# Taking the reader-less TensorE products out of the opening of a three-layer decoder kernel

## The reference, cut to what matters

```python
x = _layernorm(x + attn(x, ...))               # x: 64 sequences x 64 rows x 256
x = _layernorm(x + xattn(x, ctx, ..., 64))     # 8 heads, within |i - j| <= 64 of 256
x = _layernorm(x + ffn(x, w_gate_up, w_proj))  # ternary weights, silu(gate) * up, rms_norm

def attn(x):   # 16 heads of 16, rotary, layernorm of q and k, causal
    q = layernorm(x) @ Wq + bq; k, v = layernorm(x) @ Wkv + bkv
    q, k = ln(rotary(q)), ln(rotary(k))
    return softmax(causal(q @ k.T / 4)) @ v @ Wo + bo

def ternary_quant(w):  # groups of 64
    scale = max(mean(|w|), 1e-8); return round_to_minus1_0_1(w / scale) * scale
```

## Time and profile before

| what | value |
|---|---|
| median of 3 runs | 856.19 us |
| lowest, highest | 854.46, 863.31 us |
| the profiled execution's own time | 854.88 us |
| its span | 853.2 us |
| PE busy | 776.2 us (91%), 9593 instructions |
| DVE busy | 766.6 us (90%) |
| POOL, ACT busy | 692.5 us, 681.0 us |
| weight loads (PEld) | 464.0 us |
| share of line 538 in the chain of waits, first 220 us | 3.0% |

### The profile page before, as it was taken

The page is one execution under the profiler, slowest core; times in us unless marked ns, Lnnn a source line. Parts: engine busy times, 40 slices in busy tenths (PEclk is TensorE's granted clock), DMA queues, the critical chain, the costliest instruction groups (busy, mean ns, idle before and its releaser), DMA issues.

```text
span 853.2 us, 23669 instructions
## 1 busy us (share of the span) xinstructions
PE 776.2 (91%) x9593; PEld 464.0 (54%) x9665; DVE 766.6 (90%) x1503; ACT 681.0 (80%) x1331; POOL 692.5 (81%) x689
## 2 busy tenths in 40 slices
PE   5788899999999999999999999999999989889884
PEld 3345445555556665556666655556665556555442
DVE  5999997889999999999999999999999998889653
ACT  3367558678889899889888888999899888778864
POOL 5896578888989999999999999999999897465731
PEclk9999999899999999999999999999999999999999
DMA  8100211111333333333333333333333323334333
GB/s 263 39 25 13 58 39 40 27 35 43 70 67 62 70 77 70 76 71 76 76 66 75 67 62 70 76 74 71 67 76 71 70 64 70 70 64 82 64 76 85
DMA packets 125117, 58.00 MB, mean 68 GB/s; under 512 B 93072, under 2 KB 124048, under 8 KB 125008
## 3 DMA queue, kind: packets, MB, share of 16 engines
q1 hardware_dynamic: 125008, 56.49, 30.2%
HBM read 13.98 MB, written 4.19 MB: 21 GB/s over the span
## 4 chain that ended last, share of the span: by engine, by line
PE 69%; DVE 14%; ACT 7%; issue 3%; SPq 3%; POOL 2%; DMA 2%; POOLq 0%; DVEq 0%; ACTq 0%
PE ps L778 9%; PE ps L579 6%; PE ps L856 5%; PE ps L826 5%; PE ps L842 4%; PE ps L747 4%; PE ps L649 4%; PE ps L710 4%; PE ps L589 3%; DVE rowmax L3017 3%; PE ps L617 3%; PE ps L631 2%; PE ps L817 2%; PE ps L678 2%; PE ps L690 2%
## 5 line engine op out<-in xcount | busy, mean ns | idle before, releaser
L3017 DVE TENSOR_REDUCE rowmax<-ps 128x4 f32<-128x768 f32 x256 | 243.2, 950 | 10.1 <-PE ps L710 9.3
L1744 ACT ACTIVATE prob<-ps 128x768 f32<-128x768 f32 x256 | 207.3, 810 | 32.1 <-PE ps L747 31.9
L2508 POOL TENSOR_TENSOR hsum<-hsum,minus_half 128x32 f32<-128x32 f32 x32 | 175.9, 5495 | 11.0 <-DVE hsum L2942 10.9
L2533 POOL TENSOR_SCALAR_AFFINE_SELECT prob<-prob 128x512 f32<-128x512 f32 (+1 forms) x128 | 112.0, 875 | 24.6 <-ACT prob L1744 24.3
L2535 POOL TENSOR_SCALAR_AFFINE_SELECT prob<-prob 128x1024 f32<-128x1024 f32 (+1 forms) x128 | 114.3, 893 | 0.0
L778 PE MATMUL ps<-prob,v_pad 128*32 128x192 f32 x2048 | 97.2, 331 | 0.2 <-POOL prob L2535 0.2
L710 PE MATMUL ps<-k_rows,q_rows 31*128 31x192 f16 x1024 | 86.7, 247 | 9.1 <-DMA k_rows<-qk_lo 4.2
L747 PE MATMUL ps<-q_rows,k_rows 32*128 32x192 f16 x1024 | 86.5, 247 | 5.7 <-ACT prob L1744 5.4
L778 PEld LDWEIGHTS ps<-prob,v_pad 128*32 128x32 f32 x2048 | 60.3, 110 | 30.7 <-issue 17.1
L826 PE MATMUL ps<-wgu,xsplitT 128*128 128x512 bf16 x226 | 59.4, 380 | 12.0 <-ACT v_own L1653 9.1
L856 PE MATMUL ps<-wproj,hT 128*128 128x256 bf16 x512 | 62.5, 276 | 5.7 <-DVE y L3103 4.9
(11 more groups left out here) (162 smaller groups left out, 2025.8 us busy)
## 6 DMA issues: line engine op xcount, KB each, us to landing
v_swap<-v_own SPq DMA_DIRECT2D x64, 68.0 KB, 2.1
xin<-in_x SPq DMA_DIRECT2D x32, 128.0 KB, 2.2
enc<-in_ctx SPq DMA_DIRECT2D x32, 128.0 KB, 2.3
q_rows<-qk_hi SPq DMA_DIRECT2D x64, 64.0 KB, 2.0
k_rows<-qk_hi SPq DMA_DIRECT2D x64, 64.0 KB, 2.1
out<-yout SPq DMA_DIRECT2D x32, 128.0 KB, 2.0
prob<-in_w_guT SPq DMA_DIRECT2D x4, 512.0 KB, 6.4
q_rows<-qk_lo SPq DMA_DIRECT2D x32, 64.0 KB, 2.0
```

The costliest lines, as they stand in the source:

```text
L1744: copy(prob[:, 2 * c:2 * c + 2, :, :].rearrange("p u a b -> p u (a b)"), ps[:, STB:STB + 2, 0:2 * QW], ACT.Exp, scale=float(XD) ** -0.5).t ...
L2508: g.tensor_tensor(hsum[:, t.two, 1, :], hsum[:, t.two, 0, :], minus_half[:, :], ALU.pow).then_inc(S["head_pow3"], 1)
L2533: g.affine_select(out=lead, in_=lead, compare_op=ALU.is_ge, fill=0.0, base=BAND - 64 * kb, pattern=[[0, 8], [1, cut]], channel_multiplier=-1)
L3017: v.tensor_reduce(of_head[:, hq:hq + 2, 2 * row_of(ng):2 * row_of(ng) + 2], ps[:, MXB:MXB + 2, 0:2 * QW].rearrange("p j (a b) -> p j a b", ...
```

## The change

The function `keep_warm` and its 33 calls are removed, 165 products and 165 weight loads. All other instructions, their order and their waits stay; the lines behind move up, those of the functions by 5. Nothing changes on the other four engines. The diff, its calls cut to the first ones and the last:

```diff
@@ -532,11 +532,6 @@
                 last.then_inc(s_setup, 1)
 
-            def keep_warm(times):
-                pe.wait_ge(s_fold, 3)
-                for _ in range(times):
-                    mm(ps[:, OTB, :], identb[:, :], causal[:, :], start=True, stop=True)
-
             def sum_weights(n):
...
@@ -993,29 +988,21 @@
...
             do_qk_ps(tile[1])
-            keep_warm(5)
             sum_weights(0)
-            keep_warm(12)
             sum_weights(1)
             pe.wait_ge(S["v"], tile[0].at(1, 1))
             do_xnT_ps(tile[2])
-            keep_warm(12)
             pe.wait_ge(S["xnT"], tile[2].at(1, 1))
             do_qk_ps(tile[2])
-            keep_warm(7)
...
             do_s_ps(tile[2])
-            keep_warm(12)
             pe.wait_ge(S["s_sub"], tile[2].at(1, 1))
...
             do_mx(tile[2], 3)
-            keep_warm(3)
             pe.wait_ge(S["exp"], tile[0].at(8, 7))
```

More of the change, by code:

```diff
@@ L1009, in _ @@
             do_v_ps(tile[1])
-            keep_warm(8)
             pe.wait_ge(S["v"], tile[1].at(1, 1))
             do_s_ps(tile[0])
-            keep_warm(9)
             sum_weights(2)
-            keep_warm(10)
             pe.wait_ge(S["xn"], tile[3].at(1, 1))
             do_xnT_ps(tile[3])
-            keep_warm(6)
             pe.wait_ge(S["s_exp"], tile[0].at(1, 1))
@@ L1056, in _ @@
             sum_weights(4)
-            keep_warm(1)
             pe.wait_ge(s_vswap[tile[1].buf], tile[1].dma(2))
@@ L1134, in _ @@
             do_mx(tile[1], 1)
-            keep_warm(8)
             pe.wait_ge(S["max"], tile[1].at(8, 2))
             do_mx(tile[1], 2)
-            keep_warm(4)
             pe.wait_ge(s_vswap[tile[3].buf], tile[3].dma(2))
@@ L1147, in _ @@
             do_xproj_ps(tile[2])
-            keep_warm(2)
             pe.wait_ge(s_maxrow[tile[0].buf], tile[0].dma(1))
             do_st(tile[0], 0)
-            keep_warm(2)
             pe.wait_ge(S["max"], tile[1].at(8, 4))
```

## The result

The changed kernel took 872.5 us in the median of four runs (866.43 to 878.56), against 857.77 us for the kernel before beside it: ratio 1.0148, 95% interval 1.0087 to 1.0208. It is slower, since 1 lies outside the interval; whether by 2% is open. Every ratio and interval in this document leaves out executions more than 1.5% above the fastest one of the same kernel, while the medians given in us are over all executions. The profiled execution took 866.43 us, 11.5 us more than the profiled one of before (854.88). The calls of `keep_warm` were 32, not 33 as the text ahead says; the 165 products are right.

The account below looks back on a forecast made before the run. VectorE was taken to bound the opening. First gaps and 42 to 50 us cost 4.9 us, later falls at even chances 3.8, less 0.5 won: +8.2 on 854.88, so 863.1 us; range 853 to 873.

Parts of the forecast that it names:

- The bound and the pass-through: VectorE bounds the opening to 130 us; from 200 us both engines are full, so any loss is handed on whole.
- What it gives: VectorE's wait for tile 1's attention values at 78.58 us shrinks: 0.5 us won, bounds 0 and 6.3.
- The clock: Emptied gaps drop TensorE's clock: sure in the first two and at 42 to 50 us, even for shorter later ones.
- A: First gaps: q/k projection of tile 2 at 34.28 us runs at the low clock, VectorE waits, +1.5 us.
- B: Gaps of 42 to 50 us: transposes, tile 3's q/k projection and weight sums run slower, +3.4 us.
- C: Around 73 to 82 us: transposes, attention values and output projection slower, +2.1 us if the clock falls, at even chances.
- D: 102 to 110 us: tile 5's q/k projection and logits slower, +3.1 us if the clock falls, at even chances.
- E: 119 to 130 us: output projection and tile 6's q/k projection slower, +2.4 us if the clock falls, at even chances.
- rival 2: Clock stays low through nearly the whole opening, transposes not bringing it back: +18 us, 867 to 878 us; chance 0.17.
- rival 1: VectorE's own work hides the slower products in the opening: +0 to +4 us, 855 to 859 us; chance 0.20.
- 3 (faster): Clock does not fall in the opening and VectorE gets back 2.3 us of waits: 849 to 853 us; chance 0.08.
- 4 (nothing happens): Real work already keeps the clock level in the opening, so time stays 854.9 us; chance 0.03.

Follow-up runs that it names:

- the two half kernels: Kernel before with only blocks 10 to 32 (90 products) out: ratio 1.0131; with only blocks 1 to 9 (75) out: ratio 1.0039.

## Why the prediction was right, and where its sizes were off

**The bound and the pass-through** held. VectorE carries the opening, the engines are full from 200 to 680 us, and the lateness is handed on: 8.8 us at 182 and 9.4 at 680, between 8.2 and 9.7 on the way.

**What it gives** (0.5 us): nothing visible. The wait at 78.58 us grew from 0.51 to 1.58 us instead of shrinking.

**The clock.** "Sure in the first two gaps and in those of 42 to 50 us" held: at 24.9 and 45.4 us here, and likewise in both other kernels without the early blocks. "As even for the shorter ones later" was too low: there were three falls, at 76.1, 89.7 and 117.0 us. The reading behind it was short, too: the longest emptiness of before at the high level is not the 3.39 us of the earlier trace rows but the 4.31 us ahead of tile 30's down projection, and there the clock fell, at 842.65 us. Shown by the two half kernels: the late blocks' absence alone costs about 7.8 us up to 140 us, the early ones' about 3.1.

**A** was put at +1.5 and measured +1.6 (0.7 to 2.35 us late, of it a wait of 1.56); 1.35 was regained by 52 us, 1.0 of it because one instruction of VectorE (line 2889 of before) ran 0.73 us instead of 1.76. **B** was put at +3.4: the wait for the projection was 2.90 and that for the values 0.44, so 3.3, and the lateness grew by 2.9 between 52 and 58 us. The level did come back in time for the values (at 59.0 us), as assumed. **C**, +2.1 if it falls: it fell, +1.4 (3.8 to 5.2). **A fall at 89.7** was in no term and made +1.4 at the logits of tile 3 (5.2 to 6.6), of which 0.8 was regained by 114 us. **D**, +3.1 if it falls: the clock was 1.00 from 96.6 to 117 us and the cost nil. I had also misread: VectorE shows no wait before those logits; they ended at 109.52 us, just as it came free. **E**, +2.4 if it falls: +4.3 between 114 and 136 us, since the low level lasted 17 us and slowed the row-maximum products too, for which VectorE waited 2.1 us in one place; no price for those stood in the sum. All told 10.1 at 140 us, 8.8 at 182, against 8.2 forecast. That these are so near is partly luck: the falls behind 70 us were counted at half and three came, one of them unpriced, while D did not; 1.35 us of A and 0.8 later were regained, which the sum did not have; 0.7 us stem from before the change's place; and the 1.3 us between 140 and 182 come back because before has its own fall there.

**The remainder** is a term that I did not have. The sum stopped at 132 us and stood on one execution of before, 854.88 us, which had been lucky: its clock was 1.00 between 680 and 765 us, where seven of eight other kernels with the same end show falls. The kernel's own median over 90 executions is 860.6, 5.7 us above my base. The measured 872.5 us is 9.4 above the forecast 863.1, so this base is the larger part of it. The forecast said that "one execution can differ by as much as I forecast here" and still took 854.88 for its base. The rest, 3.7 us, is not placed: the loss itself is 8.8 us in the profiled execution, 8 to 11 between like ends and 12.7 by the ratio to before (7.5 to 17.8), against 8.2 forecast. The profiled execution is also the fastest of the changed kernel's four, and the three others had more of the lower clock (0.931 to 0.951 against 0.955); where they had it is not recorded. So the time stands near the upper end of the range (853 to 873), outside the forecast's own 859.3 to 866.9 and within what rival 2 had. By the time alone one would have picked rival 2; the trace says that it is the forecast's mechanism, and that the range held the result with half a microsecond to spare owes something to luck.

**The rivals.** 1 (VectorE's work hides it) is excluded by its waits of 13.7 us and by three falls behind 70 us. 2 (low through nearly the whole opening) did not come: the clock was low for 58 us of the opening, and came back four times before 97 us. The run from 53.5 us on held eight transposes (two groups of 1.1 us), a projection of 3.6 us and sums, and the level was back at 59.0. So the level did not stay away for the transposes' sake, which is what rival 2 needed. Whether they count toward it, as the Trainium skill denies in "TensorE: Matmul & The Clock Gate", section "PE-mode transpose", is not shown, since the projection may have brought it back, and none of my runs had transposes alone. 3 (faster) and 4 (nothing happens) are excluded. The statement of the Trainium skill, "TensorE: Matmul & The Clock Gate", section "What's actually happening", that the ramp costs under 1% of a typical kernel's span, and which would have given rival 1 or a loss under 8.6 us, is not what the centre of the measurement says, 1.5% (0.9 to 2.1), though the interval reaches below 1%. The level was lost five times in the opening here and not once.

## What to carry to other kernels

Products without a reader paid here where TensorE waits in gaps, the real work behind a gap is on the path, and the filler uses the whole array; fillers on a quarter of the rows were worse than none. Look for the gaps at both ends of a pipeline, where slots for tiles that are not there stand empty. And before a difference of 1% is forecast or explained, ask whether the profiled execution is a typical one: its mean clock beside that of the other runs tells.

## What the runs showed of the hardware that I had not expected

- The time of one and the same kernel spreads over 15 us (853.65 to 868.37 in 90 executions, each on one core, of four chips), and most of it goes with the time at the lower clock, 0.35 us for each us.
- A TensorE busy 36.92 of 40 us with products of 32 rows had a clock of 0.58 to 0.59; in the kernel before 93.60 of 110 us with whole-array products in the gaps had 1.00.
- 36 float32 products of 128 by 128 by 128, back to back from 1.11 us on, are 72 instructions: they start 213 ns apart up to 5.5 us, and 112 ns apart from 5.9 us on, when the granted clock had risen from 1.2 to 2.4 GHz at 5.8 us.
